# Sampling stage of a deformable-convolution kernel: row sums over pairs of steps, one ring for loads and hats, PSUM unloaded by VectorE

## The reference

```
xr = conv1x1(group_norm(x), w_reduce, b_reduce)
offs = conv1x1(xr, w_offset, b_offset)
off_w, off_h = (offs[:, :cm], offs[:, cm:])
f_w = deform_conv2d(xr, off_w, w_dcnw, b_dcnw)
f_h = deform_conv2d(xr, off_h, w_dcnh, b_dcnh)
...
# in deform_conv2d, for each tap and each offset group:
val = gather(y0, x0, (1 - dy) * (1 - dx)) + gather(y0, x0 + 1, (1 - dy) * dx) \
    + gather(y0 + 1, x0, dy * (1 - dx)) + gather(y0 + 1, x0 + 1, dy * dx)
out = jnp.einsum('bikhw,oik->bohw', patches, weight.reshape(Cout, Cin, KK))
```

## Time and profile before

| | |
|---|---|
| median of 3 runs | 14,181.99 us (14,181.08 to 14,190.49) |
| the profiled execution's own time | 14,182.6 us |
| its span | 14,180.8 us |
| mean granted TensorE clock | 0.957 |
| busy: TensorE, ScalarE, VectorE, GpSimd | 92%, 84%, 80%, 51% of the span |
| the changed phase, first to last sampling product | 597.9 to 9,053.5 us |

### The profile page before, as it was taken

How to read it: one execution, slowest core, us unless ns; L and a number is a source line. 1 busy time by engine, 2 the same in 40 slices (tenths; PEclk the granted TensorE clock), 3 DMA queues, 4 the chain that set the end, 5 groups by cost and what they waited for, 6 DMA issues and landing times. The chain is left out here.

```text
span 14180.8 us, 244626 instructions
## 1 busy us (share of the span) xinstructions
PE 13101.5 (92%) x80570; PEld 10384.7 (73%) x80570; DVE 11306.3 (80%) x14346; ACT 11898.4 (84%) x17151; POOL 7255.8 (51%) x3802
## 2 busy tenths in 40 slices
PE   7899999999999999999999999967168989999999
PEld 3699999999999999999999999623023335555555
DVE  4588888888887788887888888668966988888888
ACT  2499999999999999999999999616876879999998
POOL 0155555555555555555555555243320038888887
PEclk9999999999999999999999999768688889999999
DMA  4466666666666666666666666743443433333332
GB/s 108 120 169 170 168 169 168 170 168 170 168 170 168 168 170 169 170 168 167 169 169 169 169 169 170 189 121 125 146 137 107 152 131 104 103 101 104 103 101 87
DMA packets 826113, 2100.00 MB, mean 148 GB/s; under 512 B 83411, under 2 KB 440073, under 8 KB 681609
## 3 DMA queue, kind: packets, MB, share of 16 engines
q1 hardware_dynamic: 814889, 2070.18, 55.3%
q10 hardware_dynamic: 9984, 14.16, 0.3%
HBM read 1815.36 MB, written 268.74 MB: 147 GB/s over the span
## 5 line engine op out<-in xcount | busy, mean ns | idle before, releaser
L524 PE MATMUL dc_p<-dc_t 96*128 96x144 f32 x51912 | 6899.6, 286 | 30.0 <-PEq L521 29.4
L584 POOL TENSOR_TENSOR dc_t<-dc_t 128x648 f32<-128x648 f32 x2884 | 4610.4, 1599 | 4447.6 <-POOLq L583 4447.6
L524 PEld LDWEIGHTS dc_p<-dc_t 96*128 96x128 f32 x51912 | 6521.5, 189 | 76.0 <-issue 54.0
L628 DVE TENSOR_TENSOR dc_t<-dc_p,dc_t 128x1296 f32<-128x1296 f32 x2884 | 4344.3, 1506 | 879.1 <-DVEq L626 874.5
L463 ACT ACTIVATE dc_t<-dc_t 96x1152 f32<-96x1152 f32 x2886 | 3595.8, 1246 | 113.2 <-ACTq L462 111.1
L465 ACT ACTIVATE dc_t<-dc_t 96x1152 f32<-96x1152 f32 x2886 | 3360.1, 1164 | 365.1 <-ACTq L464 16.0
L2054 DVE TENSOR_TENSOR_SCAN ms_t<-ms_t,ms_p 128x512 f32<-128x512 f32 x1728 | 2128.7, 1271 | 283.5 <-PE ms_p L1996 207.0
L1970 POOL TENSOR_TENSOR ms_t<-ms_t 128x1536 f32<-128x1536 f32 x576 | 1988.0, 3457 | 504.4 <-DVE ms_t L2054 500.6
L643 DVE TENSOR_TENSOR dc_t<-dc_t 128x324 f32<-128x324 f32 x2883 | 1428.5, 495 | 799.0 <-DVEq L641 775.9
L2006 PE MATMUL ms_p<-ms_t,top_t 128*128 128x512 f32 x3456 | 1775.4, 596 | 0.0
L561 PE MATMUL dc_p<-dc_t 128*128 128x180 f32 (+1 forms) x7488 | 1661.9, 322 | 98.4 <-PEq L556 52.3
(11 more groups left out here) (208 smaller groups left out, 9834.1 us busy)
## 6 DMA issues: line engine op xcount, KB each, us to landing
dc_t<-sxd SPq DMA_DIRECT2D x1443, 864.0 KB, 5.7
ms_t<-bcd SPq DMA_DIRECT2D x576, 256.0 KB, 3.3
dc_t<-xrT SPq DMA_DIRECT2D x145, 675.0 KB, 5.6
kvd<-wk_t SPq DMA_DIRECT2D x18, 1536.0 KB, 5.1
xvd<-mi_t SPq DMA_DIRECT2D x36, 768.0 KB, 3.5
szd<-mi_t SPq DMA_DIRECT2D x36, 768.0 KB, 5.7
dld<-mi_t SPq DMA_DIRECT2D x36, 768.0 KB, 3.4
ms_t<-dld SPq DMA_DIRECT2D x36, 768.0 KB, 6.9
```

The lines of the kernel that those rows point to most:

```text
L524: ins = e.matmul(PT[j % 2][:, t // 3, (t % 3) * 144:(t % 3 + 1) * 144], HX[:, m % NHX, t * 128:(t + 1) * 128], XW[:, i, ky:ky + WIN, g * C ...
L584: e.tensor_tensor(z[:, :, 0:HALF], z[:, :, 0:HALF], z[:, :, HALF:2 * HALF], ALU.add)\
L628: e.tensor_tensor(Zt[:, n % 4, :].rearrange("p (b m i) -> p b m i", b=3, i=CG), PT[n % 2][:, :, 0:432].rearrange("p b (m i) -> p b m i", i ...
```

## The change

- The quarter-sum and the row sum are done once for two steps. `quarter` adds two neighbouring halved steps in one instruction and writes to a new tile `ZQ`; `sum_rows` adds from there into `VA`. On VectorE a step is now: unload n, then either a paired quarter-sum (of n + 3 and n + 4, odd n) or a paired row sum (of n + 2 and n + 3, even n), then weigh n + 6, then `add_up` in each tenth step.
- VectorE copies the chunks and the kept sum out of PSUM, in place of ScalarE.
- TensorE samples six steps ahead in place of four; the two PSUM tiles stay.
- `BX` goes. SP loads a pair of steps into one of eight slots of `HX`, and both hats' operations work in place there. The hats run 12 steps ahead in place of six.
- `halve` waits on odd steps for the paired row sum, and passes on two counts to TensorE; on even steps it waits for the paired quarter-sum.
- The row offsets are added in four pieces, not two, in steps 2, 4, 6 and 8; the row weights follow on ScalarE in steps 4, 5, 9 and 10. `TAB` has four buffers, `V` one.
- The tile's store is issued by ScalarE in step 3 of the next tile, in place of SP.

```diff
-    NHX, AHEAD = 8, 6
+    RP, AHEAD, LEAD = 8, 12, 6
+    EXTRA = AHEAD // 2
...
-        TAB = p.sb([128, 2, WIN + 1])
-        BX = p.sb([W, 5, 2, NPX])
-        HX = p.sb([W, NHX, NPX])
+        TAB = p.sb([128, NRB, WIN + 1])
+        HX = p.sb([W, RP, 2, NPX])
         HY = p.sb([128, 2, CM, WIN])
-        V = p.sb([128, 2, CM, WIN])
+        V = p.sb([128, CM, WIN])
         Zt = p.sb([128, 4, WIN * LEN])
+        ZQ = p.sb([128, 2, 2 * TAPS, 2 * CG])
...
-                def pair_load(j2, b, y, q):
+                def pair_load(slot, b, y, q):
+                    e.wait_ge(s_free, 1).then_inc(s_free, -1)
                     src = k.d["sxd"][b, DS(y, 1)].rearrange("a c (q k) x -> (a c q) (k x)", q=5)
                     src = src[q:q + 1, :].partition_broadcast(W)
-                    e.dma_start(BX[:, j2 % 5, :, :].rearrange("p u n -> p (u n)"), src)\
-                        .then_inc(s_bx[j2 % 5], 16)
+                    e.dma_start(HX[:, slot, :, :].rearrange("p u n -> p (u n)"), src).then_inc(s_bx[slot], 16)
...
-                    e.activation(BX[:, q, u, :], BX[:, q, u, :], ACT.Abs, bias=QX[:, 0:1]).then_inc(s_ab, 1)
+                    e.activation(HX[:, q, u, :], HX[:, q, u, :], ACT.Abs, bias=QX[:, 0:1]).then_inc(s_ab, 1)
                     e.wait_ge(s_ab, 1).then_inc(s_ab, -1)
-                    e.activation(HX[:, slot, :], BX[:, q, u, :], ACT.Relu, bias=1.0, scale=-1.0)\
-                        .then_inc(s_hx, 1)
+                    e.activation(HX[:, q, u, :], HX[:, q, u, :], ACT.Relu, bias=1.0, scale=-1.0).then_inc(s_hx, 1)
...
                 def body(b, y2, w):
                     for n in range(NBB):
-                        e.wait_ge(s_tr, 1).then_inc(s_tr, -1)
-                        if n % NG == 1:
-                            keep_sum((n - 11) // NB % 2, n // NG % 2 ^ 1)
-                        for u, c in enumerate(pieces[n % NG]):
-                            o = min(128, NG * LEN - 128 * c)
-                            ins = e.activation(VT[0:o, n % 2, u, :], PR[0:o, u * 128:(u + 1) * 128], ACT.Copy)
-                        ins.then_inc(s_vt, 1)
-                        m = (n + AHEAD) % NBB
-                        hats(m % NB, m % NHX)
-                        if 14 <= n % NB < 18:
-                            row_weights((n // NB + 1) % 2, n % NB - 14)
+                        i, j = n // NB, n % NB
+                        if j == 3:
+                            y = y2 * NRB + i
+                            done = b * NT + y if i else e.snap(((w + 15) >> 4) * NRB + (b * NT + y))
+                            store_tile((i - 1) % NRB, done, s_st[(i - 1) % 2])
+                        hats((n + AHEAD) % NBB)
+                        if j in (4, 5, 9, 10):
+                            row_weights((i + 1) % 2, (4, 5, 9, 10).index(j))
...
-                        if g == 1:
-                            ins = turn_sum((n - 11) // NB % NRB, conv ^ 1)
+                        if g == 2:
+                            ins = turn_sum((n - 12) // NB % NRB, conv ^ 1)
                         ins.then_inc(s_tr, 1)
-                        sample(m)
+                        sample((n + LEAD) % NBB)
...
                     if n >= 2:
-                        e.wait_ge(s_sum, 1).then_inc(s_sum, -1)
-                        e.sem_inc(s_va, 1)
+                        if n % 2:
+                            e.wait_ge(s_sum, 1).then_inc(s_sum, -1)
+                            e.sem_inc(s_va, 2)
+                        else:
+                            e.wait_ge(s_qt, 1).then_inc(s_qt, -1)
...
+                def unload(n):
+                    e.wait_ge(s_tr, 1).then_inc(s_tr, -1)
+                    if n % NG == 2:
+                        keep_sum((n - 12) // NB % 2, n // NG % 2 ^ 1)
+                    for u, c in enumerate(pieces[n % NG]):
+                        o = min(128, NG * LEN - 128 * c)
+                        ins = e.tensor_copy(VT[0:o, n % 2, u, :], PR[0:o, u * 128:(u + 1) * 128])
+                    ins.then_inc(s_vt, 1)
...
                 def quarter(n):
 
-                    e.wait_ge(s_half, 1).then_inc(s_half, -1)
-                    z = Zt[:, n % 4, :].rearrange("p (t m) -> p t m", t=TAPS)
-                    e.tensor_tensor(z[:, :, 0:2 * CG], z[:, :, 0:2 * CG], z[:, :, 2 * CG:4 * CG], ALU.add)\
-                        .then_inc(s_qt, 1)
+                    e.wait_ge(s_half, 2).then_inc(s_half, -2)
+                    z = Zt[:, n % 4:n % 4 + 2, :].rearrange("p s (t m) -> p (s t) m", t=TAPS)
+                    e.tensor_tensor(ZQ[:, n // 2 % 2, :, :], z[:, :, 0:2 * CG], z[:, :, 2 * CG:4 * CG], ALU.add)\
+                        .then_inc(s_qt, 2)
...
                 def body(b, y2, w):
-                    for n in range(4, NBB + 4):
-                        weigh(n)
-                        quarter(n - 1)
-                        if n % NG == 3:
-                            add_up(b, (n - 13) // NB, (n - 13) // NG % 2)
-                        sum_rows(n - 2)
-                        if n % NB in (15, 16):
-                            rows((n // NB + 1) % 2, n % NB - 15)
+                    for n in range(NBB):
+                        m = n + 5
+                        unload(n)
+                        if m % NB in (7, 9, 11, 13):
+                            rows((m // NB + 1) % NRB, (m % NB - 7) // 2)
+                        if m % 2 == 0:
+                            quarter(m - 2)
+                        else:
+                            sum_rows(m - 3)
+                        weigh(m + 1)
+                        if n % NG == NG - 1:
+                            add_up(b, n // NB, n // NG % 2)
```

More of the change, by code:

```diff
@@ L431, in body @@
                         for q in range(10):
-                            e.wait_ge(s_bxf, 1).then_inc(s_bxf, -1)
+                            pair_load((10 * i + q) % RP, b, y, q)
                             if q == 0:
                                 tile_load(i, b, first)
[L435 to L439, removed]
                 loops(e, body)
                 row_loads(0, 0, 0, 0)
[L443 to L452, removed]
+                for q in range(EXTRA):
+                    pair_load(q, 0, 0, q)
+                    if q == 0:
+                        tile_load(0, 0, 0)
+                e.wait_ge(s_free, RP + 2 - EXTRA).then_inc(s_free, EXTRA - 2 - RP)
             @blk.scalar
@@ L456, in _, with hats @@
                 e.wait_ge(s_wr[0], 1).then_inc(s_wr[0], -1)
[L458 to L460 removed]
+                def hats(m):
+                    q, u = m // 2 % RP, m % 2
                     if u == 0:
                         e.wait_ge(s_bx[q], 16).then_inc(s_bx[q], -16)
[L463 removed]
+                    e.activation(HX[:, q, u, :], HX[:, q, u, :], ACT.Abs, bias=QX[:, 0:1]).then_inc(s_ab, 1)
                     e.wait_ge(s_ab, 1).then_inc(s_ab, -1)
[L465 to L466 removed]
+                    e.activation(HX[:, q, u, :], HX[:, q, u, :], ACT.Relu, bias=1.0, scale=-1.0).then_inc(s_hx, 1)
                 def row_weights(i, step):
@@ L481, in _ @@
                 for step in range(4):
                     row_weights(0, step)
[L483 to L491, removed]
+                for m in range(AHEAD):
+                    hats(m)
@@ L535, in turn_sum @@
                     return ins
-                sample(0)
-                sample(1)
-                for j in range(2, 4):
+                for m in range(2):
+                    sample(m)
+                for m in range(2, LEAD):
                     e.wait_ge(s_pt, 1).then_inc(s_pt, -1)
-                    sample(j)
+                    if m % 2:
+                        e.sem_inc(s_free, 1)
+                    sample(m)
+                e.wait_ge(s_pt, 1).then_inc(s_pt, -1)
                 def body(b, y2, w):
                     for n in range(NBB):
-                        j, m = n % NB, (n + 4) % NBB
+                        j = n % NB
                         conv, g = j // NG, j % NG
@@ L566, in body @@
                         elif j % 2 == 0:
-                            ins.then_inc(s_bxf, 1)
+                            ins.then_inc(s_free, 1)
                 loops(e, body)
@@ L588, in body @@
                     for n in range(NBB):
-                        halve(n + 4)
-                for n in range(4):
+                        halve(n + 5)
+                for n in range(5):
                     halve(n)
                 loops(e, body)
+                e.wait_ge(s_z, 1).then_inc(s_z, -1)
             @blk.vector
@@ L617, in add_up, with keep_sum @@
                     a = ACC[:, i, conv, :]
-                    e.scalar_tensor_tensor(out=a, in0=a, scalar=TAB[:, i % 2, WIN:WIN + 1],
+                    e.scalar_tensor_tensor(out=a, in0=a, scalar=TAB[:, i, WIN:WIN + 1],
                                            in1=PF[:, conv * CM:(conv + 1) * CM], op0=ALU.mult, op1=ALU.add).then_inc(s_ff, 1)
+                def keep_sum(i, conv):
```

(40 more changed lines are left out.)

46 lines of the change are left out of this document (22 added, 24 removed).

## The result

The changed kernel takes 13,784.7 us (median of 4 runs, 13,775.4 to 13,787.9), the kernel before 14,185.7 (4 runs): a ratio of 0.9716, 95% interval 0.9699 to 0.9733. It is faster by 401 us. The forecast was 13,780, in a range of 13,690 to 14,010.

What follows compares the result with a forecast made beforehand. The GpSimd–VectorE ring was taken to set 2.932 us a step; the change brings TensorE's 2.775 plus 0.015, 2.79: 409 us off, 4 on, from 14,182.6 to 13,780 us, range 13,690 to 14,010.

Steps and rivals of the forecast that it cites:

- TensorE's floor: TensorE's own need in the sampling stage, from record spacings: 55.5 us a tile, 2.775 us a step.
- The ring: GpSimd–VectorE cycle before the change: halving, quarter-sum, row sum, next halving; 2.81 us a step, 57.9 of 58.6 a tile with extras.
- the additions: L616 and L618 on VectorE, between quarter-sum and row sum twice a tile before the change: +1.1 us a tile.
- The paired ring: GpSimd–VectorE cycle over two steps after the change: 5.04 us in plain pairs, against TensorE's 5.55.
- ScalarE's share: Rest of the old 58.6 us tile beyond 57.9, put down to unloadings queued behind row weights, sometimes late for the convolution.
- the sum of loads: ScalarE's work a tile after losing 26 unloadings and gaining one DMA issue: 54.1 us at most, below TensorE's 55.5.
- Sizes on VectorE: Instruction times after the change: copies 0.28 us, quarter-sums 0.84, row sums 0.495; VectorE 49.0 us a tile.
- No new wait for the copies: Sampling six ahead on two PSUM tiles adds no wait; the loop through unloading takes 5.2 us, under 5.55.
- What stays: Waits behind additions and kept sums after the change: 0.015 us a step above 2.775, making 2.79.
- the signs of being wrong: Trace signs: weighings with no idle time before them, halvings well over 1.6 us, or idle time before hats.
- the harmless wait: ScalarE waits once a tile for the sum kept on VectorE, with hats for six steps or more in hand (16 us).
- The rival of contention: VectorE sums contend with GpSimd halvings; 1.8 to 2.4 us a tile stay, about 14,040 to 14,130 us; chance 0.17.

Runs made afterwards that it cites:

- e8: Changed kernel with the running total taken from the accumulator one step later, so TensorE is released one addition earlier: 13,756 us, ratio 0.9695.
- e12: The kernel with the running total taken one step later, run once more beside the unaltered changed kernel: 13,752 us, ratio 0.9705.
- e2: Kernel before, with eight of nine sampling products in each step of the loop: 14,149 us, ratio 0.9987.
- e3: Changed kernel, with eight of nine sampling products in each step of the loop: 13,517 us, ratio 0.9542.
- e9: Kernel before, single sums, with VectorE unloading directly behind a weighing and the additions moved there too, both ahead of the quarter-sum: 14,098 us, ratio 0.9951.
- e1: Kernel before, with GpSimd's halving done for only 5 of the 9 taps: 14,044 us, ratio 0.9913.
- e5: Changed kernel, with unloading and the kept sum back on ScalarE and a tick on VectorE after each weighing: 13,835 us, ratio 0.9761.
- e4: Kernel before, single sums, with VectorE unloading at the head of its step, ahead of the weighing, and ten HX buffers: 14,473 us, ratio 1.0211.
- e10: Changed kernel, with the hats 8 steps ahead in place of 12: 13,781 us, ratio 0.9725.

## Why the prediction was right

**TensorE's floor.** Right. 2.775 from spacings, 2.774 in e8 and e12. e2 and e3 show what it stands for: the same edit is worth 0.1% before and 1.8% after.

**The ring.** Right, and shown. Two halvings of the kernel before that follow each other:

```profile
4039.59 1.56 POOL L584 TENSOR_TENSOR dc_t<-dc_t 128x648 f32<-128x648 f32 x1 [1.80 <-POOLq L583]
...
4042.39 1.58 POOL L584 TENSOR_TENSOR dc_t<-dc_t 128x648 f32<-128x648 f32 x1 [1.24 <-POOLq L583]
```

They start 2.80 apart. Averaged by step over the stage, the distance is 2.81 or 2.82 us in 13 of a tile's 20 steps, and 3.13 in the two with row offsets; the other 1.8 us a tile lie in the five steps around the additions, where the prediction had 1.1 for the additions and 0.7 for ScalarE. e9, in which TensorE and ScalarE have room, runs at 57.9 us a tile. That this is the very number of the prediction is in part luck: in e9 the row steps cost 0.8, the additions, which stand elsewhere there, 0.6, and other steps 0.35, where the prediction added 0.62 and 1.1. The paired ring was right too, and e3, which runs against it, shows its terms: by the starts of its halvings a plain pair of steps takes 5.11 us (forecast 5.04), one with a row piece 5.55 (5.49), with a kept sum as well 5.70 (5.8), and one at the additions 5.49 (5.6).

**ScalarE.** Right in kind, and too small. I read the 0.7 us between 57.9 and 58.6 as ScalarE's share, as if it were the next term of a sum. They were two bounds side by side: with the ring short, ScalarE's list and its waits hold the kernel at 57.6 (e1), without ScalarE's part the ring holds it at 57.9 (e9). Taking one away is worth 0.5 to 0.9%; the change, which takes both away, 2.8%. That the forecast came out right needed both to be gone, which the change does and the sum of loads (54.1 us at most for ScalarE) said.

**What gave how much.** Of 2.8%, everything but the copies gives 2.4 (e5) and the copies 0.4. Inside the 2.4 lies a part that is ScalarE's too: 57.6 us in e1, 56.1 in e5. Of these 1.5 us a tile the traces place 1.2: 0.9 are waits for loads, which e5, with loads further ahead and the image rows behind a pair's load, doesn't have, and 0.3 waits ahead of the kept sums. The last 0.3 could come from the spread of the row weights or from the two steps' more room for an unloading; no run changes one of these parts alone, so their worth in time isn't shown. With samples only four ahead, VectorE's order of steps would make a pair's row sum after the unloading that waits for its transposes, so pairs without the two steps more weren't run.

**Sizes on VectorE.** Copies 0.281 (0.28 forecast), quarter-sums 0.829 (0.84), row sums 0.488 (0.495), kept sum 0.409 (0.41: 0.33 net and the overlap of 0.08). Only the row pieces were off: 0.663 on average against some 0.53. VectorE's busy time is 7,322 / 144 = 50.8 us a tile, forecast 49.0; the pieces are some 0.5 of the difference.

**No new wait for the copies.** Right, and e4 shows what that step was worth: with four steps ahead and the copies behind the sums the same move is a loss of 2.1%. What made it harmless is its place, directly behind a weighing and ahead of the sums: in the timeline the transposes run at 4,036.42, the copy at 4,037.83 and the convolution at 4,038.74. That two more steps of lead aren't needed for it is shown by e9, which has four.

**What stays.** 0.015 us a step was put down to additions and kept sums. The step measured is 2.786, so 0.011 above the floor, and e8 takes it away by releasing TensorE one addition earlier. The DMA share went to 0.70 (forecast 0.71), with no wait for loads on TensorE. ScalarE does stand idle before hats, which the prediction named among the signs of being wrong: 116.9 us of 2,000, at the store that waits for the sum kept on VectorE (L473). TensorE waits for no hat in that time, and shortening the lead changed nothing (e10), so it is the harmless wait that the prediction had described.

**What the forecast left out.** The first tile takes 66.7 us, where the later ones take 55.7, and where it took 56.7 before. The row data of the second tile, which are now needed in step 2, are issued at 619.5 behind the loads that fill the ring of eight, and land at 640.7. The first row piece waits for them, and TensorE behind it:

```profile
640.80 0.53 DVE L596 TENSOR_TENSOR dc_t<-dc_t 128x360 f32<-128x360 f32 x1 [11.12 <-DVEq L594]
...
643.71 1.54 PE L544 MATMUL dc_p<-dc_t 128*128 128x180 f32 x4 [10.63 <-PEq L539]
```

The forecast had 4 us for the start and nothing for this. The residue, 0.011 in place of 0.015 us a step, gave 12 us back. So the mechanism was right, and that the forecast is only 5 us off is in part luck: two errors of some 11 us cancel. The stage ends at 8,659 us and not near 8,640; the forecast's own sum, 9,053 less 405, makes 8,648.

**The rival of contention.** Its mechanism is there, its price isn't. Of 143 row pieces in 2,000 us, 107 start while a halving runs and take 0.71 on average; the other 36 take 0.52:

```profile
4041.01 0.52 DVE L596 TENSOR_TENSOR dc_t<-dc_t 128x360 f32<-128x360 f32 x1
...
4045.10 1.56 POOL L570 TENSOR_TENSOR dc_t<-dc_t 128x648 f32<-128x648 f32 x1 [1.25 <-POOLq L569]
...
4046.36 0.70 DVE L596 TENSOR_TENSOR dc_t<-dc_t 128x360 f32<-128x360 f32 x1
```

The halving is 1.57 throughout. Three pieces a tile lose 0.19 each, 0.6 us a tile, and VectorE had it to spare: it still waits 107 us of the 2,000 for samples.

## What to carry to other kernels

Find a loop's floor on an engine from the spacing of records that wait for nothing, not from its busy share: 98% busy hid 5% here. When two cycles of nearly equal length bind, removing one shows only the small difference between them (0.5 and 0.9% here, of 2.8); add up every cycle, waits for loads included, to its own period before you say what a part is worth. A moved instruction is paid by its place in the new queue more than by its length: with the same 0.2 us copies on VectorE the kernel was 2.1% slower when they stood behind the sums, and 0.5% faster when they stood behind the weighing, with the additions moved there too.

## What was not expected of the hardware

Which engine pays when VectorE and GpSimd both read two tensors from SBUF depended, in these traces, on which started first. Before, L609 ran when the halving started, and the halving took 1.89 us in place of 1.57. After, the halving ran when L596 started at 4,046.36 (it ended at 4,046.66), and L596 took 0.70 in place of 0.52. In 143 instances of L596 between 4,000 and 6,000 us the shortest is 0.516 and the longest 0.996, while 718 halvings lie between 1.551 and 1.594; in the same stretch before, all 68 instances of L609 started first and took 0.90, and the halvings beside them 1.88 on average. The Trainium skill, "SBUF — State Buffer", section "Who interferes with whom", states that a VectorE instruction with two SBUF inputs contends with a GpSimd instruction that reads SBUF, and that the order of issue decides who blocks. The traces agree in direction; the time lost (0.18 of an overlap of 0.30, 0.32 of an overlap of 0.46) is less than the whole overlap, where the page has an exclusive lock.
